# Role adapter with layer norm on one core: the first transfers of batch 0 split up and spread over two queues

## The reference, cut to what matters

```python
h = jnp.einsum('bsh,bhk->bsk', hidden_states, W_down[role]) + b_down[role][:, None, :]
h = jax.nn.gelu(h, approximate=False)
u = jnp.einsum('bsk,bkh->bsh', h, W_up[role]) + b_up[role][:, None, :]
y = hidden_states + u
mean = jnp.mean(y, axis=-1, keepdims=True)
var = jnp.mean(jnp.square(y - mean), axis=-1, keepdims=True)
yn = (y - mean) * jax.lax.rsqrt(var + LN_EPS)
return yn * gamma[role][:, None, :] + beta[role][:, None, :]
```

## Time and profile before

| | us |
|---|---|
| median of 3 runs (363.91 to 364.08) | 364.08 |
| the profiled execution, its own time | 363.8 |
| its span, first to last instruction | 362.0 |
| TensorE busy in the span | 353.3 |

### The profile page before, as it was taken

One profiled execution on the slowest core, in us unless ns is written; L12 is line 12 of the kernel. 1 busy time (PEld: TensorE's weight loads), 2 busy tenths in 40 slices (PEclk: granted clock), 3 DMA queues, 4 the chain that ended last, 5 costly groups with the idle time before them and its releaser, 6 DMA issues.

```text
span 362.0 us, 4935 instructions
## 1 busy us (share of the span) xinstructions
PE 353.3 (98%) x1548; PEld 289.7 (80%) x1548; DVE 286.0 (79%) x296; ACT 183.5 (51%) x295; POOL 59.2 (16%) x73
## 2 busy tenths in 40 slices
PE   8999999999999999999999999999999999999992
PEld 4888888888888888888888888888888888888881
DVE  3796889678995899778996699957989668994776
ACT  4793545871367515673356714476225871345131
POOL 0000132003220213102140023200232003220012
PEclk9999999999999999999999999999999999999999
DMA  7999999983999649894699918999199982654023
GB/s 211 414 409 408 381 310 349 351 304 86 339 326 358 224 131 383 273 362 184 203 376 309 364 81 274 355 327 352 49 313 347 357 293 77 213 176 173 0 116 117
DMA packets 27227, 96.59 MB, mean 267 GB/s; under 512 B 3154, under 2 KB 3410, under 8 KB 27218
## 3 DMA queue, kind: packets, MB, share of 16 engines
q1 hardware_dynamic: 23040, 81.80, 63.9%
q10 hardware_dynamic: 4178, 14.69, 10.3%
HBM read 79.70 MB, written 16.78 MB: 267 GB/s over the span
## 4 chain that ended last, share of the span: by engine, by line
PE 96%; DMA 1%; DVE 1%; SPq 0%; issue 0%; ACT 0%; DVEq 0%
PE down_ps L268 48%; PE up_ps L275 48%; DMA wd_stage<-W_down 1%; DVE h_full L573 0%; DMA roles_sb<-roles 0%; DVE rows L579 0%; DVE up_ps L556 0%; SPq L149 0%; ACT wd_hi L459 0%; DVEq L42 0%; DVE last_mean L566 0%; DVE neg_shift L564 0%; SPq L238 0%; DVEq L555 0%
## 5 line engine op out<-in xcount | busy, mean ns | idle before, releaser
L268 PE MATMUL down_ps<-x_hi,wd_hi 128*128 128x512 f32 x256 | 81.6, 390 | 0.6 <-ACT wd_hi L459 0.6
L268 PE MATMUL down_ps<-x_lo,wd_hi 128*128 128x512 f32 x256 | 81.4, 389 | 0.0
L268 PE MATMUL down_ps<-x_hi,wd_lo 128*128 128x512 f32 x256 | 81.4, 389 | 0.0
L275 PE MATMUL up_ps<-wu_hi,h_hi 128*128 128x512 f32 x256 | 79.5, 389 | 0.0
L275 PE MATMUL up_ps<-wu_hi,h_lo 128*128 128x512 f32 x256 | 79.4, 389 | 0.0
L275 PE MATMUL up_ps<-wu_lo,h_hi 128*128 128x512 f32 x256 | 79.4, 389 | 0.0
L477 POOL TENSOR_TENSOR var_eps<-var,eps 128x1 f32<-128x1 f32 x31 | 22.1, 714 | 292.7 <-ACT squares L386 292.7
L383 ACT ACTIVATE neg_mean_scaled<-row_sum 128x1 f32<-128x1 f32 x31 | 6.3, 202 | 114.4 <-DVE rows L540 114.4
L268 PEld LDWEIGHTS down_ps<-x_hi,wd_hi 128*128 128x128 f32 x256 | 47.9, 188 | 11.2 <-issue 1.3
L275 PEld LDWEIGHTS up_ps<-wu_hi,h_hi 128*128 128x128 f32 x256 | 48.0, 188 | 10.0
L268 PEld LDWEIGHTS down_ps<-x_lo,wd_hi 128*128 128x128 f32 x256 | 48.0, 188 | 10.0
(11 more groups left out here) (46 smaller groups left out, 232.4 us busy)
## 6 DMA issues: line engine op xcount, KB each, us to landing
wu_stage<-W_up SPq DMA_DIRECT2D x32, 512.0 KB, 7.1
rows<-x SPq DMA_DIRECT2D x32, 512.0 KB, 6.6
x_stage<-xT SPq DMA_DIRECT2D x31, 512.0 KB, 6.7
wd_stage<-W_down SPq DMA_DIRECT2D x31, 512.0 KB, 6.6
out<-rows ACTq DMA_DIRECT2D x28, 512.0 KB, 4.7
b_up_row<-b_up SPq DMA_DIRECT2D x8, 512.0 KB, 4.8
gamma_row<-gamma SPq DMA_DIRECT2D x8, 512.0 KB, 9.1
beta_row<-beta SPq DMA_DIRECT2D x8, 512.0 KB, 9.8
```

The costliest lines, as they stand in the source:

```text
L268: return pe.matmul(down_ps[:, kc, :], wd_part[:, n, c * K + kc * P:c * K + (kc + 1) * P], x_part[:, n, c * S:(c + 1) * S], start=start, st ...
L275: mm = pe.matmul(up_ps[:, t % 2, half], h_part[:, kc, t * P:(t + 1) * P], wu_part[:, kc, half], start=(kc == 0 and h_part is h_hi and wu_p ...
```

## The change

It touches batch 0 alone (and the order in which batch 1's first x part is rounded).

- The first EARLY = 256 of W_down's columns in the first chunk of part 0 are loaded for all three roles by ScalarE's queue, at the place where `b_down_all` was loaded, into the space of `rows` tile 0. VectorE reads the role, copies the role's own 256 columns into `wd_hi` (which rounds them) and subtracts for `wd_lo`. SyncE then waits for `early_wd_lo` before it loads `rows` tile 0.
- SyncE loads the other 256 columns of that chunk and, after the first x part, W_down only: part 1 in two chunks, parts 2 and 3 whole.
- ScalarE's queue loads x's part 1 in two chunks and parts 2 and 3 whole, between its own roundings, and `b_down_all` after them.
- Rounding, splitting and the matmuls of parts 0 and 1 go chunk by chunk, with semaphores for each. The very first chunk is computed in two halves: blocks `kc` 0 and 1 in all three passes, then `kc` 2 and 3.
- In batch 0, part 2 is computed for all `kc` ahead of part 3, and only part 3 goes block by block.
- One dummy matmul less. In `first_steps`, x part 0 of batch 1 is rounded and split ahead of the first Gelu's h.

```diff
-    WARM_UP = 12
+    WARM_UP = 11
+    EARLY = K // 2
...
+        early_wd = rows[:, 0, 0:R * EARLY]
...
+                elif t == 0:
+                    sp.wait_ge(early_wd_lo, 1)
...
+            load_first_x(0, first_x_landed[0])
+            load_first_x(1, x_landed[0])
             sp.wait_ge(roles_landed, 16)
             first_role = load_role(sp, 0)
-            sp.dma_start(wd_stage[:, 0, 0:K], wd_src(first_role)[:, 0, 0:K]).then_inc(first_wd_landed, 16)
-            sp.dma_start(wd_stage[:, 0, K:CPL * K], wd_src(first_role)[:, 0, K:CPL * K]).then_inc(wd_landed[0], 16)
-            for i in range(1, NLOAD):
-                load_x_part(0, i)
+            load_first_wd(0, 0, first_wd_landed[0], skip=EARLY)
+            load_first_wd(0, 1, wd_landed[0])
+            load_first_wd(1, 0, first_wd_landed[1])
+            load_first_wd(1, 1, wd_landed[1])
+            for i in range(2, NLOAD):
                 load_wd_part(first_role, i)
...
+            def first_chunk():
+
+                pe.wait_ge(first_x_hi, 1)
+                for early in (True, False):
+                    kcs = range(KC // 2) if early else range(KC // 2, KC)
+                    for down_pass in range(len(PASSES)):
+                        if down_pass == 0:
+                            pe.wait_ge(early_wd_hi if early else first_wd_hi, 1)
+                        elif down_pass == 1:
+                            pe.wait_ge(first_x_lo, 1)
+                        else:
+                            pe.wait_ge(early_wd_lo if early else first_wd_lo, 1)
+                        for kc in kcs:
+                            down(0, 0, kc, down_pass, start=(down_pass == 0))
...
+                if first:
+                    pe.wait_ge(x_split, NLOAD - 1)
+                    pe.wait_ge(wd_split, NLOAD - 1)
+                    for kc in range(KC):
+                        for c in range(CPL):
+                            for down_pass in range(len(PASSES)):
+                                down(NLOAD - 2, c, kc, down_pass)
                 for kc in range(KC):
-                    for n in range(NLOAD // 2, NLOAD):
+                    for n in range(NLOAD - 1 if first else NLOAD // 2, NLOAD):
...
             act.dma_start(roles_sb[:, :], roles).then_inc(roles_landed, 16)
-            act.dma_start(b_down_all[:, :], b_down_cols).then_inc(b_down_landed, 16)
+            act.dma_start(early_wd.rearrange("p (r k) -> p r k", r=R),
+                          W_down.rearrange("r (n p c) k -> p n c r k", n=NLOAD, c=CPL)[:, 0, 0, :, 0:EARLY]).then_inc(early_wd_landed, 16)
...
+            round_first(x_hi, x_stage, 0, c0, first_x_landed[0], first_x_hi)
+            load_first_x(1, c0, first_x_landed[1])
+            round_first(x_hi, x_stage, 0, c1, x_landed[0], x_hi_ready)
+            load_first_x(1, c1, x_landed[1])
+            round_first(wd_hi, wd_stage, 0, slice(EARLY, K), first_wd_landed[0], first_wd_hi)
+            round_first(wd_hi, wd_stage, 0, c1, wd_landed[0], wd_hi_ready)
+            load_first_x(2, slice(0, CPL * S), x_landed[2])
+            round_first(x_hi, x_stage, 1, c0, first_x_landed[1], first_x_hi)
+            round_first(wd_hi, wd_stage, 1, c0, first_wd_landed[1], first_wd_hi)
+            load_first_x(3, slice(0, CPL * S), x_landed[3])
+            act.dma_start(b_down_all[:, :], b_down_cols).then_inc(b_down_landed, 16)
+            round_first(x_hi, x_stage, 1, c1, x_landed[1], x_hi_ready)
+            round_first(wd_hi, wd_stage, 1, c1, wd_landed[1], wd_hi_ready)
...
+            def split_first_part():
+                dve.wait_ge(roles_landed, 16)
+                own = early_wd[:, bass.ds(load_role(dve, 0) * EARLY, EARLY)]
+                dve.wait_ge(early_wd_landed, 16)
+                dve.tensor_copy(wd_hi[:, 0, 0:EARLY], own).then_inc(early_wd_hi, 1)
+                split_first(x_lo, x_stage, x_hi, 0, slice(0, S), first_x_hi, first_x_lo)
+                dve.wait_ge(early_wd_hi, 1)
+                dve.tensor_tensor(wd_lo[:, 0, 0:EARLY], own, wd_hi[:, 0, 0:EARLY].bitcast(F32),
+                                  ALU.subtract).then_inc(early_wd_lo, 1)
```

More of the change, by code:

```diff
@@ L168, in _ @@
         def _(sp):
-            def x_src(batch):
-                return xT[batch].rearrange("(n p c) s -> p n (c s)", n=NLOAD, c=CPL)
             def wd_src(role):
@@ L285, in steps @@
                     parts = NLOAD * b + n + 1
-                    chunks_apart = first and n == 0
+                    if first:
+                        if n == 0:
+                            first_chunk()
+                        else:
+                            chunk(n, 0)
+                        mm = chunk(n, 1)
+                        mm.then_inc(d_part_used, 1)
+                        continue
                     for down_pass in range(len(PASSES)):
-                        if down_pass == 0 and not chunks_apart:
+                        if down_pass == 0:
                             pe.wait_ge(x_hi_ready, parts)
@@ L349, in round_wd_part, with round_first @@
                 act.copy(wd_hi[:, i, :], wd_stage[:, i, :]).then_inc(wd_hi_ready, 1)
+            def round_first(hi, stage, i, chunk, landed, ready):
+                act.wait_ge(landed, 16)
+                act.copy(hi[:, i, chunk], stage[:, i, chunk]).then_inc(ready, 1)
             def round_next_x(b, i):
@@ L405, in first_steps @@
                     round_wu(0, i)
+                round_next_x(0, 0)
                 gelu(0, 0, role)
[L407 to L410, removed]
+                round_wd_part(1, 0)
+                for kc in range(1, KC):
+                    gelu(0, kc, role)
                 round_next_part(0, 1)
@@ L519, in split_wd_part, with split_first @@
                                   ALU.subtract).then_inc(wd_split, 1)
+            def split_first(lo, stage, hi, i, chunk, hi_ready, ready):
+                dve.wait_ge(hi_ready, i + 1)
+                dve.tensor_tensor(lo[:, i, chunk], stage[:, i, chunk], hi[:, i, chunk].bitcast(F32),
+                                  ALU.subtract).then_inc(ready, 1)
+            def split_first_part():
[7 more added lines that the diff above has]
+                                  ALU.subtract).then_inc(early_wd_lo, 1)
+                split_first(wd_lo, wd_stage, wd_hi, 0, slice(EARLY, K), first_wd_hi, first_wd_lo)
+                split_first(x_lo, x_stage, x_hi, 0, slice(S, CPL * S), x_hi_ready, x_split)
+                split_first(wd_lo, wd_stage, wd_hi, 0, slice(K, CPL * K), wd_hi_ready, wd_split)
             def split_wu(b, i):
@@ L601, in first_steps @@
                     split_wu(0, i)
+                split_x_part(1, 0)
                 split_h(0, 0)
-                split_x_part(1, 0)
                 split_wd_part(1, 0)
-                split_h(0, 1)
-                split_h(0, 2)
-                split_h(0, 3)
+                for kc in range(1, KC):
+                    split_h(0, kc)
                 bias_tile(0, 0)
@@ L669, in _ @@
             dve.memset(squares[:, 0:BANK], 0.0).then_inc(zeros_ready, 1)
-            for i in range(NLOAD):
+            split_first_part()
+            split_first(x_lo, x_stage, x_hi, 1, slice(0, S), first_x_hi, first_x_lo)
+            split_first(wd_lo, wd_stage, wd_hi, 1, slice(0, K), first_wd_hi, first_wd_lo)
+            split_first(x_lo, x_stage, x_hi, 1, slice(S, CPL * S), x_hi_ready, x_split)
+            split_first(wd_lo, wd_stage, wd_hi, 1, slice(K, CPL * K), wd_hi_ready, wd_split)
+            for i in range(2, NLOAD):
                 split_x_part(0, i)
```

48 lines of the change are left out of this document (32 added, 16 removed).

## The result

The kernel before took 364.13 us (median of 6 runs), the changed one 366.91 us (median of 6, from 365.75 to 368.66): a ratio of 1.0082 with a 95% interval of 1.0068 to 1.0097. It is slower by 0.8%, outside the forecast range, and its runs spread more widely than those of before. The profiled execution is the slowest of the six: 368.66 us, with a span of 366.8.

The account below looks back on a forecast made before the run. TensorE was taken as the bound, busy 353.3 of a 362.0 us span. Start -0.53 and first stretch +0.13 gave -0.40: 363.4 against the profiled 363.8, or 363.7 against the median; range 363.1 to 364.8.

Parts of the forecast that it names:

- the landing of the early columns: W_down's first 256 columns of all roles, issued at 1.29, land at 5.5, between 4.9 and 6.2.
- the term of the first matmul: Start of batch 0's down product: first real matmul at 5.96 against 6.49, 0.53 us won.
- the slow beginning on a tensor not yet read: Early DMA: a half stretch moving only 193 GB/s; half of this delay was counted in the landing at 5.5.
- the paragraph on the dummies: Before the first real matmul: eleven dummies end near 5.7, leaving about 0.3 us idle, at no cost.
- D: SyncE's W_down chunks share the engines, early columns land at 6.2, first matmul at 6.66: 364.4 us; chance 0.12.
- Everything behind 28.67 runs at TensorE's pace: After batch 0's down product: TensorE sets the pace, the tail follows, and the diff touches neither.
- 21.76: Time in us of each stretch of 96 matmuls behind up's start; any other value would make the prediction wrong.
- the copy: VectorE's copy of the role's own 128x256 early columns, which rounds them: 0.30 us.
- the order of the Gelus: End of batch 0's down product: last block is split 3.1 us after it, due at 4.08; no cost.
- The stall for x_lo: First chunk: TensorE waits 0.21 us for x_lo, there at 6.70, plus a restart of some 0.1.
- Rival C: x's part 2, issued by ScalarE behind SyncE's backlog, lands at 14.5: +1.1 us, 364.5 to 364.8; chance 0.20.
- limit of 13.5: Time by which x's and W_down's part 2 must have landed for TensorE to reach part 2 without waiting.

Follow-up runs that it names:

- a_near: Changed kernel with the early columns' three pieces read from one role's matrix, 2 KB apart (values not the role's): 365.46 us, ratio 1.0038.
- b_warm8: Kernel before with 8 dummy matmuls in place of 12, no DMA changed: 365.71 us, ratio 1.0034.
- second profile: From the changed kernel run once more, unchanged: 366.42 us, ratio 1.0060; the profiled execution took 367.69.
- a_own_spx: Changed kernel with early columns of the own role only, loaded by SyncE, and x's parts 1 to 3 issued by SyncE: 364.17 us, ratio 0.9995.
- a_own_spx_order: a_own_spx with reordered work on ScalarE and VectorE in batch 0, and h's splits ahead of bias additions in every batch: 363.13 us, ratio 0.9965.
- a_own: Changed kernel with early columns of the own role only, loaded by SyncE behind the role read (131 kB for 393 kB): 365.87 us, ratio 1.0037.
- a_own_x2early: a_own with ScalarE issuing x's parts 2 and 3 right behind part 1, not between the later casts: 364.34 us, ratio 1.0021.
- a_512k: Changed kernel with the early columns' three pieces read from one role's matrix, 512 KB apart (values not the role's): 365.49 us, ratio 1.0035.
- a_warm17: Changed kernel with 17 dummy matmuls in place of 11, nothing else: 366.15 us, ratio 1.0044.
- a_hold: Changed kernel with SyncE issuing no W_down until the early columns of all roles have landed: 370.03 us, ratio 1.0158.
- a_spx_warm17: Changed kernel with 17 dummies and x's parts 1 to 3 by SyncE, early columns of all roles kept on ScalarE's queue: 365.33 us, ratio 1.0035.

## Why the prediction was wrong

The sum gave 363.7 us and a gain of 0.4; measured were 366.9 and a loss of 2.8.

**The step that failed first** is the landing of the early columns, "at the rate of a full stretch ... 0.95 us more", 5.5 between 4.9 and 6.2. It was 7.3, and the term of the first matmul, -0.53, became +1.42. The rate came from stretches in which each transfer read one place; while three matrices 2 MB apart were being read, all transfers together moved 152 and 156 GB/s. With the same bytes, pieces and queue from one matrix the sum was right (5.6, a_near). I had named the slow beginning on a tensor not yet read, and not asked what three separate matrices would do to it. Whether it is that slow beginning three times over or the distance stays open. W_down's other half chunk, which I had "landed whole by 5.70 before", shared the delay: its cast came at 7.75.

**The second** is the paragraph on the dummies: "Eleven end near 5.7 and leave an idle of about 0.3 ... No cost." It rested in part on the first. The eleven ended at 6.05 in one profile and 5.59 in the other, and with a landing of 7.3 to 7.8 the idle stretch was 1.86 and 2.78 us. The real matmuls began at the low level in both: in the first it had never risen, in the second it had risen and fell. That cost 2.8 and 1.6 us. I priced the late landing only by the time it is late (D: 364.4). The Trainium skill, "TensorE: Matmul & The Clock Gate" (Part 1), says that the low level is the default and activity lifts it. Both profiles and b_warm8 agree in kind, and that rule should have been joined to D.

**The third** is the sentence "Everything behind 28.67 runs at TensorE's pace". The changed kernel already breaks it, by the wait of 0.7 us before 76.80 (0.2 in its second profile), though it starts later than the kernel before; its stretch of 22.05 is not the 21.76 that I had made a condition. a_own_spx, with a start earlier than before, breaks it twice. The kernel before has neither wait, and I had no row that showed how near it is to them. Why the `rows` of batch 1 come too late in the changed kernel too is not shown; that the order of VectorE's work decides whether it costs anything is (a_own_spx_order).

**Right, within its bounds:** the copy (0.30 forecast, 0.29 to 0.30 measured), the hand-over (0.14), the start near 5.96 when the columns land near 5.45 (5.90 in a_own, 5.95 in a_own_spx_order), the order of the Gelus and the splits of the first chunk. The stall for x_lo was smaller than forecast: the third matmul came 0.54 behind the first in a_own_spx_order, where the sum had 0.74, and its first stretch took 22.11, less than the 22.3 I had.

**Rival C** was right in mechanism. Its limit of 13.5 fits, but was not tested closely: a cast of part 2 from 13.14 cost nothing (a_own_x2early), casts from 14.93 on did (a_512k and later). It cost time in every version whose x part 2 is issued late by ScalarE (a_warm17, a_own, a_near, a_512k, a_hold), but for the changed kernel, whose slow matmuls covered it; the chance of 0.20 was too low. Its price was 1.1 in my working and 0.85 to 1.96 in the runs. My own sum had it "just in time", and the deciding instruction stood behind a cast that itself waited for a DMA; a delay of the one is a delay of the other.

## What to carry to other kernels

A start that waits for a DMA has two prices, the lateness and the clock lost by the idle time ahead of it, so the number of dummies should follow the time at which the data is really there: 17 that left 1.3 us of idle kept the clock in two profiles, 11 that left 1.9 to 2.8 did not. A transfer issued from an engine's instruction stream inherits each wait of that stream, and here was under way for some 7 us beside a full SyncE queue. When an early gain does not show at the end, look for the first wait of the bounding engine behind it: two changes of order that are worth nothing on the old kernel were worth 1.0 us together on the one that starts earlier.

## What the runs showed of the hardware

A transfer of 393 kB in pieces of 1 KB took 4.3 us from one matrix and 5.9 to 6.5 from three matrices 2 MB apart, with or without SyncE's W_down chunks beside it. Between 4 and 5 us the engines then moved 118 GB/s (a_hold) to 179 GB/s (a_spx_warm17), and with one matrix 361 and 368. Two executions of the same kernel ran their first real matmuls at the low clock for 8 and for 14 matmuls, behind 2.78 and 1.86 us of idle. In a_hold 1.95 us of idle were followed by five matmuls at the upper level, and the low one came at 8.93. With 8 dummies for 12, the kernel before lost 0.34% (0.18 to 0.51%).
